# A two-layer attention kernel: numerators and denominators in one TensorE pass, aligned by transfers

## The reference

```python
# x: (64, 64, 128), ctx: (64, 128, 128), mask: (64, 128) int
x = x + xattn(layernorm(x), ctx, ctx, mask)      # 16 heads of 8, causal, key mask
x = x + attn(layernorm(x))                        # latent k and v of width 32
x = x + ffn(layernorm(x))                         # 8-bit quantized, exact gelu
# xattn: softmax(where(mask == 0 or k > q, -inf, q @ k.T / sqrt(8))) @ v, then @ Wo
# attn:  s = clip(q @ k.T * scale) * decay(|i - j|); softmax(s) @ v, then @ Wo
```

## Time and profile before

| | |
|---|---|
| median of 3 runs | 310.6 us (310.31 to 310.81) |
| profiled execution | 311.19 us, its span 309.4 us, mean granted clock of PE 0.989 |
| busy share | PE 92%, DVE 83%, ACT 71%, POOL 68% |
| chain that ended last | PE 73%, DVE 15%, issue 4%, DMA 3% |
| sums by ones (L612) | 40.0 us busy |
| feed-forward part | from about 268 us to 309.4 us |

### The profile page before, as it was taken

One profiled execution on the slowest core, in us unless ns is written; L12 is line 12 of the kernel. 1 busy time (PEld: TensorE's weight loads), 2 busy tenths in 40 slices (PEclk: granted clock), 3 DMA queues, 4 the chain that ended last, 5 costly groups with the idle time before them and its releaser, 6 DMA issues.

```text
span 309.4 us, 13624 instructions
## 1 busy us (share of the span) xinstructions
PE 285.5 (92%) x5744; PEld 197.6 (64%) x5744; DVE 255.9 (83%) x558; ACT 219.6 (71%) x496; POOL 209.9 (68%) x167
## 2 busy tenths in 40 slices
PE   7789879999999999999999999999999999699593
PEld 2356547676767777675767686777777768332282
DVE  2898679999888888888888787878888998789873
ACT  3585856575768876666777778788857877699590
POOL 5676557777877766799999998988799962230000
PEclk9999999999999999999999999999999999999869
DMA  8999000101010000000000000000000000000027
GB/s 229 313 286 298 12 28 4 36 2 40 2 37 9 31 19 20 28 14 24 17 33 6 21 20 21 19 21 20 11 31 5 2 5 4 0 0 0 2 78 195
DMA packets 19038, 15.05 MB, mean 49 GB/s; under 512 B 5985, under 2 KB 15522, under 8 KB 18978
## 3 DMA queue, kind: packets, MB, share of 16 engines
q1 hardware_dynamic: 18258, 13.75, 15.5%
q10 hardware_dynamic: 720, 0.43, 0.5%
HBM read 8.67 MB, written 2.10 MB: 35 GB/s over the span
## 4 chain that ended last, share of the span: by engine, by line
PE 73%; DVE 15%; issue 4%; DMA 3%; ACT 2%; POOL 1%; SPq 1%; DVEq 0%; ACTq 0%; POOLq 0%
PE ps L579 12%; PE ps L560 11%; PE ps L606 10%; PE ps L612 8%; PE ps L622 8%; DVE hmax L1108 6%; PE ps L577 4%; PE ps L495 4%; PE ps L487 4%; PE ps L474 3%; PE ps L591 3%; DVE u L1027 3%; PE ps L718 2%; DMA arena<-in_mask_BxS_if 2%; DMA out<-pt 1%
## 5 line engine op out<-in xcount | busy, mean ns | idle before, releaser
L829 ACT ACTIVATE pt<-ps 128x512 f32<-128x512 f32 x128 | 76.0, 595 | 30.5 <-PE ps L579 23.3
L408 POOL TENSOR_TENSOR u<-u,mx 128x1024 f32<-128x1024 f32 x32 | 60.8, 1902 | 35.3 <-DVE mx L1046 35.1
L400 POOL TENSOR_TENSOR ud<-u,con 128x1024 f32<-128x1024 f32 x31 | 73.4, 2367 | 6.6 <-DVE u L1032 6.5
L1027 DVE SCALAR_TENSOR_TENSOR u<-ps,rs,arena 128x1024 f32<-128x1024 f32 x32 | 40.9, 1279 | 14.1 <-PE ps L560 12.7
L1032 DVE TENSOR_SCALAR u<-ps 128x1024 f32<-128x1024 f32 x32 | 39.0, 1220 | 11.8 <-PE ps L560 11.3
L560 PE MATMUL ps<-arena,qT 32*64 32x256 f32 x1024 | 44.0, 399 | 4.9 <-DVE u L1027 2.5
L606 PE MATMUL ps<-pt,vx 128*32 128x64 f32 x2048 | 41.4, 221 | 2.9 <-DVE oT L968 1.3
L606 PEld LDWEIGHTS ps<-pt,vx 128*32 128x32 f32 x2048 | 32.5, 110 | 16.4 <-issue 11.5
L612 PE MATMUL ps<-pt,con 128*32 128x128 f32 x1024 | 40.0, 273 | 0.7 <-issue 0.7
L1046 DVE TENSOR_REDUCE mx<-u 128x16 f32<-128x1024 f32 x32 | 38.7, 1210 | 0.1
L834 ACT ACTIVATE lden<-ps 128x128 f32<-128x128 f32 x64 | 17.7, 277 | 29.5 <-PE ps L612 29.4
(11 more groups left out here) (153 smaller groups left out, 513.5 us busy)
## 6 DMA issues: line engine op xcount, KB each, us to landing
arena<-kT SPq DMA_DIRECT2D x52, 64.0 KB, 2.2
out<-pt SPq DMA_DIRECT2D x8, 256.0 KB, 2.8
arena<-in_ctx_cols SPq DMA_DIRECT2D x4, 256.0 KB, 4.5
xn3T<-in_x_cols SPq DMA_DIRECT2D x4, 256.0 KB, 4.6
x<-in_x SPq DMA_DIRECT2D x4, 256.0 KB, 5.2
arena<-in_ctx_cols SPq DMA_DIRECT2D x2, 512.0 KB, 6.3
xn3T<-in_x_cols SPq DMA_DIRECT2D x2, 512.0 KB, 6.0
x<-in_x SPq DMA_DIRECT2D x2, 512.0 KB, 7.3
```

Of the source, the lines that this page charges most:

```text
L400: pool.tensor_tensor(dh, uh, decay.unsqueeze(1).to_broadcast([P, H, HALF]), ALU.mult)\
L408: pool.tensor_tensor(uh, uh, mx[:, n % 4, 0:count].unsqueeze(2).to_broadcast([P, count, HALF]), ALU.subtract)\
L829: act.activation(pt[:, n % 2, 4 * half:4 * half + 4].rearrange("p h n -> p (h n)"), ps[:, bank, :], ACT.Exp).then_inc(s["emptied"], 1)
L1027: dve.scalar_tensor_tensor(by_head(u[:, n % UB]), sc, rs[:, 0, n:n + 1], mask[:, n].unsqueeze(1).to_broadcast([P, H, HALF]), ALU.mult, ALU ...
```

## The change

The value columns in `vx` are widened. For each pair of heads the 32 columns that PE loads now hold a value column and a column of ones by turns, so that one pass writes numerators and sums. A head of one parity writes columns 0 to 127 of the bank, of the other parity 128 to 255; a sum lies one row from its numerator. The product with ones goes away, save for the last two tiles (`WHOLE`), which keep the old form in a buffer of their own (`vl`).

ACT copies the 256 columns out of PSUM (`take_out`, a new instruction a tile) and SP issues four transfers of 64 rows by 512 bytes that move sums and numerators into matching rows (`align`, semaphores `D_IN` and `N_IN`, three slots). The logarithm, inverse and division of a tile come a turn later than before, the residual too. On ACT the logarithm of a tile stands ahead of `take_out` of the next one. In layer one `divide` is POOL's, ahead of its subtraction; in layer two it is DVE's, with the inverse in PSUM.

The integers of the mask are loaded as two rows in one transfer instead of broadcast copies. DVE turns them into bfloat16, and PE spreads each eight tiles' part over the rows and adds the causal part (a piece "m", four in all), which ACT copies out. `make_mask` is gone from POOL. DVE clears two thirds of `vx` at the start; POOL writes the ones in twelve small instructions. SP's key transfers are split over two turns each and put in one order with `align`. Some turn numbers (`ROOT_TURN`, `APPLY3`) move by one.

```diff
-MASKS = ((0, 4), (4, 8), (8, 16), (16, 32))
-LAG_T, LAG_SHIFT, LAG_PV, LAG_ADD = 2, 3, (3, 4), (4, 5)
+LAG_T, LAG_SHIFT, LAG_PV, LAG_DEN = 2, 3, (3, 4), (4, 5)
+WHOLE = NS - 2
...
+def den_turn(n):
+    return n + (LAG_PV[1] if n >= WHOLE else LAG_DEN[n // NT])
+def divided(turn):
+    return [n for n in range(NS) if den_turn(n) == turn]
+def added(turn):
+    return [n for n in range(NS) if den_turn(n) + 1 == turn]
...
+            def align(n):
+                slot = n % RAW
+                sp.wait_ge(s["raw_done"], n + 1)
+                if n >= RAW:
+                    product_made(sp, n - RAW)
+                sp.dma_start(nd[0:P:2, slot, 1], raw[1:P:2, slot, 0]).then_inc(D_IN[slot], 16)
+                sp.dma_start(nd[1:P:2, slot, 1], raw[0:P:2, slot, 1]).then_inc(D_IN[slot], 16)
+                sp.dma_start(nd[0:P:2, slot, 0], raw[0:P:2, slot, 0]).then_inc(N_IN[slot], 16)
+                sp.dma_start(nd[1:P:2, slot, 0], raw[1:P:2, slot, 1]).then_inc(N_IN[slot], 16)
...
+                for tile in divided(n):
+                    if tile < NT:
+                        divide(tile)
...
                 if 1 <= n < NS - 1:
-                    pe.wait_ge(s["o_ready"], n)
+                    pe.wait_ge(s["raw_done"], n)
+                if NT + 2 <= n < NS - 1:
+                    product_made(pe, n - 2)
+                if n < WHOLE:
+                    for b in range(2):
+                        for par in range(2):
+                            for r in range(RG):
+                                last = pe.matmul(ps[32 * r:32 * (r + 1), bank, P * par + HALF * b:P * par + HALF * (b + 1)],
+                                                 vx[:, j % RING3, b, i, r, 32 * par:32 * (par + 1)],
+                                                 pt[:, n % 2, 2 * r + par, HALF * b:HALF * (b + 1)], start=True, stop=True)
+                    last.then_inc(s["pv_done"], 1)
+                    return
...
+            def take_out(n):
+                act.wait_ge(s["pv_done"], n + 1)
+                if n >= RAW:
+                    act.wait_ge(D_IN[n % RAW], aligned(n - RAW))
+                    act.wait_ge(N_IN[n % RAW], aligned(n - RAW))
+                act.copy(raw[:, n % RAW].rearrange("p a n -> p (a n)"), ps[:, OB, 0:2 * P])\
+                    .then_inc(s["raw_done"], 1)
...
             def log_den(n):
-                act.wait_ge(s["pv_done"], n + 1)
-                act.activation(lden[:, n % 2], ps[:, num_den(n), P:2 * P], ACT.Ln).then_inc(s["ln_done"], 1)
+                if n < WHOLE:
+                    act.wait_ge(D_IN[n % RAW], aligned(n))
+                    act.activation(lden[:, n % 2], nd[:, n % RAW, 1], ACT.Ln).then_inc(s["ln_done"], 1)
...
+                for tile in divided(n):
+                    if tile < WHOLE:
+                        log_den(tile)
                 for tile in due(n, LAG_PV):
-                    log_den(tile)
+                    if tile < WHOLE:
+                        take_out(tile)
...
+            dve.wait_ge(s["mask_in"], 16)
+            dve.tensor_scalar(mask_b[:, :], mask_i, 0.0, MASKED, ALU.is_equal, ALU.mult).then_inc(s["mask_cast"], 1)
```

More of the change, by code:

```diff
@@ L104, in ring_plan @@
         pieces[n] += these
+    for c in range(1, NT // MASK_TILES):
+        pieces[MASK_TURN[c]].append(("m", c))
     for n in range(NS):
@@ L116, in ring_plan @@
         keys = [("t", turn - LAG_T, half) for half in range(2)] if 0 <= turn - LAG_T < NS else []
-        order += [("o", n) for n in due(turn, LAG_ADD)] + keys + pieces[turn]
+        order += [("o", n) for n in added(turn)] + keys + pieces[turn]
         by_act += [("t", n, 1) for n in [turn - LAG_SHIFT] if NT <= n < NS] + (keys if turn - LAG_T < NT else keys[:1]) + pieces[turn]
@@ L224, in perceiver_block @@
         KX_IN = [s[f"kx_in{n}"] for n in range(RING3)]
-        MASK_IN = [s[f"mask_in{n}"] for n in range(4)]
+        N_IN, D_IN = [s[f"n_in{n}"] for n in range(RAW)], [s[f"d_in{n}"] for n in range(RAW)]
         STORED = [s[f"stored{n}"] for n in range(4)]
@@ L261, in gelu_count, with aligned, columns_of @@
             return 1 + max(m for m, e in enumerate(GELUS) if e[0] == k)
+        def aligned(n):
+            return 32 * (n // RAW + 1)
+        def columns_of(v, slot, e, first, between):
+            pitch, blocks = v.shape[1] * v.shape[2] * v.shape[3] * RG * VW, v.shape[3] * RG
+            return [bass.AP(v[:, :, :, :, :, :].tensor, HALF * e * pitch + (2 * slot + b) * blocks * VW + 2 * DH * e + first,
+                            [[pitch, HALF], [VW, blocks], [between, 2], [2, DH]]) for b in range(2)]
         def gets_empty(what):
@@ L410, in _ @@
                         .then_inc(s["shifted"], 1)
-                for m, (turn, _, _, _) in enumerate(MAKE):
-                    if turn == n:
-                        make_mask(m)
                 for turn, k, m in NMRS:
@@ L458, in piece @@
                         last = pe.transpose(ps[:, bank, i * P:(i + 1) * P], src[:, i], ident)
+                if kind == "m":
+                    if j == 0:
+                        pe.wait_ge(s["mask_cast"], 1)
+                        pe.wait_ge(s["pair_cast"], 1)
+                        pe.wait_ge(s["causal_cast"], 1)
+                        pe.wait_ge(s["ident_cast"], 1)
+                    bank = bank_of(what)
+                    pe.matmul(ps[:, bank, :], pair_b[:, :], mask_b[:, j * MASK_TILES * HALF:(j + 1) * MASK_TILES * HALF],
+                              start=True, stop=False)
+                    last = pe.matmul(ps[:, bank, :], ident_b[:, :],
+                                     causal_b[:, :].unsqueeze(1).to_broadcast([P, MASK_TILES, HALF]), start=False, stop=True)
                 if kind == "cq":
@@ L651, in _ @@
                     values(tile)
-                for tile in due(n, LAG_ADD):
+                for tile in added(n):
                     project(tile)
@@ L772, in piece @@
                     last = act.copy(xT[:, j % 2], ps[:, bank, :])
+                if kind == "m":
+                    last = act.copy(mask[:, j * MASK_TILES:(j + 1) * MASK_TILES].rearrange("p t k -> p (t k)"), ps[:, bank, :])
                 if kind == "cq":
@@ L1047, in _ @@
                             .then_inc(s["maxed"], 1)
-                for tile in due(n, LAG_PV):
-                    if tile not in (EARLY, NS - 1):
+                for tile in divided(n):
+                    if NT <= tile < NS - 1:
                         divide(tile)
@@ L1060, in _ @@
                     variance(0, i)
[L1061 to L1067 removed]
+                if 0 <= n - LAG_MOMENTS < NT:
+                    moments(1, n - LAG_MOMENTS)
+                if 0 <= n - LAG_MOMENTS - 1 < NT:
+                    variance(1, n - LAG_MOMENTS - 1)
+                for i in moments3(n):
+                    moments(2, i)
+                for i in variances3(n):
+                    variance(2, i)
                 if n == NS - 1 + LAG_PV[1]:
```

173 lines of the change are left out of this document (108 added, 65 removed).

## The result

The kernel after takes 328.8 us (median of 4, 326.6 to 330.6) against 310.7 before: 1.0578 times as long, interval 1.0513 to 1.0644. The forecast was 299.6 with a range of 292 to 307. The profiled execution took 328.63 us with a span of 326.8.

What follows compares the result with a forecast made beforehand. PE was taken to bound the kernel from turn 8 through layer two, with DVE and POOL just under it. Terms -0.7 + 2.3 + 4.7 + 4.7 + 0 = 11.0 us off 310.6 gave 299.6, range 292 to 307.

Steps and rivals of the forecast that it cites:

- PE's saving: On PE, dropping the sums saves 0.60 us a turn in layer one and 0.33 in layer two.
- The terms -2.3, -4.7 and -4.7: Forecast changes in us for turns 8 to 17, turns 18 to 31 and turns 32 to 62.
- PE's own limit: Turns 18 to 31: PE's 3.74 us a turn less 0.60 leaves 3.14.
- DVE's term: Turns 8 to 17: DVE loses the division, 0.28 us a tile; 35.4 in place of 37.7, gain 2.3.
- The closed cycle: Copy, SP's issue, landing, logarithm, next copy, once a turn: 3.3 us in layer one, 3.5 in layer two.
- covered by a turn of 3.4: SP's queue: four transfers and on average one key transfer a turn, 2.4 to 3.0 us of issuing, hidden.
- The rival of the other side: Slower than before: alignment slow, the cycle passes the old turn from 3.8 us; 318 to 333 us, chance 0.11.
- POOL's floor of 3.70: Turns 32 to 62: POOL's work, four more divisions and gaps, some 115 us for 119.4; gain 4.7.
- ACT's load: ACT with 0.38 us of copy a turn: 43 of 47.6 and 103 of 117 us, about 90%, covered thinly.
- The start: Before turn 8: first moments 3.6 us late at about 10.1, partly regained; turn 8 0.7 us later.
- The end: Last turns: transfers add about 3 us, PE's savings and the late turn shorten; zero, between -1.5 and +2.

Runs made afterwards that it cites:

- pass by itself: Kernel before with only PE's new pass writing both bank halves, no sums, alignment or mask; every second head's values left out: 296.4 us, 0.9547.
- changeover mended: As logarithm last, but the divisions of tiles 28 to 31 are made by DVE instead of POOL: 316.1 us, 1.0161.
- logarithm last: Changed kernel with ACT doing the copy first, then both exponentials, then logarithm and inverse of the older tile: 317.5 us, 1.0244.
- changeover and end mended: As changeover mended, and the last four tiles instead of two take the old way (sums on PE, no transfers): 313.7 us, 1.0056.

## Why the prediction was wrong

**PE's saving: right in sum, not part by part.** The terms -2.3, -4.7 and -4.7, made from the 0.60 of a sums' pass and the floors below it, give 11.7 us. The pass by itself gained 14.0, in the two profiled spans 15.1: 3.0 before turn 8, 0.8, 3.6 and 6.4 in the three groups of turns, 1.3 at the end. The gain before turn 8 I had put down as covered. The 0.8 does not test the 2.3, which came from DVE's division, and that stays on DVE in this kernel. For turns 18 to 31 I had PE's own limit at 3.14; with PE full in it (51.04 of 52) the pass ran at 3.48 a turn. From the start of the values to that of the projection PE took 1.02 us before and 0.58 now (at 102.48 and at 103.90), 0.44 less and not 0.60. Layer two gained more than I gave it. That the sum came out so near is in part luck. And DVE's term holds a slip: 33.0 + 2.2 is 35.2 and not 35.4, and that stands for the 38 us of the stretch, so by its own reasoning the gain was 2.8.

**The closed cycle: the right mechanism, mis-sized. This is the step that failed.** I wrote 3.3 us for it in layer one, 3.5 in layer two, and called SP's queue "covered by a turn of 3.4". Turns 18 to 31 took 55.96 / 14 = 4.00, turns 32 to 62 took 125.29 / 31 = 4.04. Two errors, both to be seen in the pieces of the way round. First, the landing went in as a typical one, 2.1 us. A closed cycle passes every late landing on, so its mean counts, and that was 2.41 with a median of 2.15; over the whole kernel the median was 1.9, but seven landings after the first lay between 3.1 and 3.9. The Trainium skill, DMA: Bandwidth & Descriptors, section "Anatomy of one DMA", calls its 2.0 us constant, for transfers that GpSimd issues; for these, which SyncE issues, the trace agrees with the 2.0 at the median only (1.8 to 1.9) and not with a constant. Second, the queue was priced as an average: one key transfer a turn. They come two at a time, and such a turn takes SP 3.83 us. That queue is the same cycle's, since the alignment of the next tile is issued behind it: the copy was ready 0.30 us in the mean before SP took it up, where I had 0.06. Changing ACT's order and halving the transfers each gave 11 us back, and together little more. In turns 18 to 31 the new order gave back 5.3 us of the 8.3 missed. In turns 32 to 62 it gave back 2.3 of the 10.6, and 4.8 with the changeover mended; the other 5.8 there stay open. The rival of the other side, that the cycle passes the old turn from 3.8 us on, is what happened, at 0.11; its 318 to 333 holds the result, though it had asked for a landing of 2.6 or more.

**POOL's floor of 3.70 in layer two: close as a floor, not the limit.** The pass by itself, without the four divisions, ran at 112.96 / 31 = 3.64 a turn there. In the changed kernel POOL was busy 109.32 of 122 us, less than before. What I had seen of it was the sum of its work (1.9 us for four more divisions), not their place: behind 2.33 us of decay, with PE waiting for the result. At the changeover alone that made a turn of 8.7 us in the better order.

**ACT's load: right as a sum.** "43 of 47.6": with the logarithm last ACT is busy 44.63 us in 52. In that kernel turns 18 to 31 take 3.62 and turns 32 to 62 take 3.97, though the profile shows no large wait of ACT for a transfer.

**The start: wrong, +3.8 for +0.7.** The first moments at 8.58 were earlier than the 10.1 that I had expected, since the mask had landed by 7.17 and not 7.92, and the cast took 1.48 and not 2.2. I had said that the late start hides the first alignment's wait behind the loads; ACT waited 2.93 us for it, and work at the lower clock on PE behind it made turn 5 last 9.5 us. With the logarithm last turn 8 is at 42.3, before the old 42.73.

**The end: wrong, +3.4 for 0.** The last projection is 16.3 us behind turn 63 instead of 12.7. I had set the chain of copy, landing, logarithm and inverse against PE's savings. That chain is not shown to be the cause: with the last four tiles in the old form, without transfers and without the added turn of lag, the distance stayed 16.5. What I had overlooked is a place in a queue again. In the changed kernel the last tile's inverse is ready at 280.04 and its division begins at 282.19, since DVE is at the last norms' work; in the kernel before it was 264.02 and 264.54. That is 1.6 us of the 3.6; the rest is open.

**What stays open.** The changed kernel lost 32.4 us against the pass alone. ACT's order explains 11, the changeover some 2.6. Of the rest, some 16 to 19 us, the starts of the turns show where it lies, in the kernel with changeover and end mended against the pass alone: 3.2 up to turn 8, 1.4 in turns 8 to 17, 2.3 in turns 18 to 31, 6.3 in layer two, 3.4 at the end. ACT's copy (0.36 us, 62 times), the added turn of lag and the lower clock after PE's gaps may be in it; I have not separated them.

## What to carry to other kernels

When a fixed latency is put into a loop that closes on itself once a turn, price the loop by the mean of that latency with its late cases in it, and by the full length of its queue in the worst turn, not by a median and an average load; and before that, see whether the instruction that waits can stand last in its engine's order, which here was worth 11 us for a few moved lines. An engine that idles after the change is no proof of a gain: ask of each wait who is queued behind it, and who waits for those. When a division, a copy or a conversion moves to another engine, its place in that queue at the seams (layer change, start, last turns) counts more than its duration.

## What the runs showed of the hardware

Small transfers between rows of the chip's own memory (32 KB, 64 pieces of 512 bytes) are even in the middle and have a long tail: landing 1.8 us in the median and, once the loads are over, up to 3.9, issue 0.6 us and up to 1.9. Of 248 such transfers 42 landed later than 2.6 us and 24 took over 0.8 us to issue.

The late ones do not lie at random. About every 8 us the chip moves 16 KB of instructions in one transfer of 0.9 to 1.5 us (38 in this span), as beside the slow issue at 104.89 (the DMA queues from 103.6 to 105):

```profile
q1 hardware_dynamic: 136, 0.06, 14.6%
q8 instruction: 1, 0.02, 6.6%
```

In the trace of the changed kernel 99 of the 248 transfers have such an instruction transfer under way between the start of their issue and their landing, and 41 of them land late; of the other 149 one does. All 24 slow issues overlap one too. The same count gives 42 of 105 against 1 of 143 with the logarithm last, and 13 of 27 against 0 of 25 for the key transfers of the kernel before. So a late landing hardly occurs without an instruction transfer beside it, though more than half of those that have one are in time. No run changed the instruction traffic, so that it is the cause is not shown; it is the first thing to test.

The clock fell when PE had been made to wait: after the 2.85 us at the first logarithm and after the 2.78 at the changeover it ran at the lower level for several microseconds. In the stretch from 10 to 42 us the granted clock was 0.84, where the kernel before had 1.00; one part of that lies behind the first logarithm, another from 10 to 14 us (0.71), where PE had just waited 2.22 us for the mask's conversion and had done little before. Not every wait did this: behind the 2.54 us at the end (267.92 in the kernel with the end edit) the projection took 0.49 us, behind 2.84 at the same place with the logarithm last 0.80. So a wait on PE can cost more than its own length.
